# A four-layer mixture of experts on one core: the next layer's first weights scaled by ScalarE and split by VectorE one expert at a time, and the bias sums moved to another bank

## The reference, cut to what matters

```python
def _moe_layer(x, rw, rb, g, b, w1, b1, w2, b2):
    probs = softmax(einsum('bsh,he->bse', x, rw) + rb)
    vals, idx = top_k(probs, 2);  vals = vals / vals.sum(axis=-1, keepdims=True)
    xhat = normalized x (mean 0, variance 1 over h)
    xe = xhat[None] * g[:, None, None, :] + b[:, None, None, :]
    h = gelu(einsum('ebsh,ehf->ebsf', xe, w1) + b1[:, None, None, :])
    y = einsum('ebsf,efh->ebsh', h, w2) + b2[:, None, None, :]
    return sum over e of comb[e] * (x + y[e])     # comb: vals of the chosen two, else 0
for l in range(4): x = _moe_layer(x, rw[l], ..., b2[l])
```

## Time and profile before

| what | us |
|---|---|
| median of 3 runs (2304.45 to 2312.71) | 2306.93 |
| the profiled execution: its own time | 2305.76 |
| its span, first to last instruction | 2303.9 |
| TensorE busy in the span | 2152.2 (93%) |
| VectorE busy | 2023.0 (88%) |
| ScalarE busy | 1515.3 (66%) |
| GpSimd busy | 957.7 (42%) |
| expert stage, from TensorE's first product of it | some 916 |

### The profile page before, as it was taken

One profiled execution on the slowest core, in us unless ns is written; L12 is line 12 of the kernel. 1 busy time (PEld: TensorE's weight loads), 2 busy tenths in 40 slices (PEclk: granted clock), 3 DMA queues, 4 the chain that ended last, 5 costly groups with the idle time before them and its releaser, 6 DMA issues. The chain is left out here.

```text
span 2303.9 us, 49912 instructions
## 1 busy us (share of the span) xinstructions
PE 2152.2 (93%) x16960; PEld 1272.2 (55%) x16960; DVE 2023.0 (88%) x2878; ACT 1515.3 (66%) x1794; POOL 957.7 (42%) x464
## 2 busy tenths in 40 slices
PE   7887999999999999999999998998999999989987
PEld 3342333333333333333333347987899889989976
DVE  5768999999999999999999997777877877787776
ACT  4767888888888888888888873433344334434432
POOL 3224344443434444344434434444444544444442
PEclk9986999999999999999999999998999999999998
DMA  5886122212222221212222133000100010000000
GB/s 171 242 247 176 40 46 41 45 39 49 42 45 46 41 46 39 45 41 48 44 42 46 41 105 110 1 0 0 38 1 0 2 37 0 0 1 6 5 9 19
DMA packets 354955, 114.91 MB, mean 50 GB/s; under 512 B 283000, under 2 KB 345600, under 8 KB 354624
## 3 DMA queue, kind: packets, MB, share of 16 engines
q1 hardware_dynamic: 350416, 110.92, 19.6%
q10 hardware_dynamic: 4464, 3.02, 0.4%
HBM read 67.98 MB, written 45.88 MB: 49 GB/s over the span
## 5 line engine op out<-in xcount | busy, mean ns | idle before, releaser
L1492 DVE TENSOR_TENSOR_SCAN arena<-behind 128x1040 f32<-128x1040 f32 x512 | 1156.9, 2309 | 7.8 <-ACT behind L971 5.1
L1040 ACT ACTIVATE arena<-PS,arena 128x512 f32<-128x512 f32 x512 | 348.7, 688 | 545.6 <-PE PS L1272 544.7
L961 ACT ACTIVATE behind<-PS 128x1024 f32<-128x1024 f32 x512 | 526.7, 1029 | 133.8 <-DVE arena L1492 101.8
L1175 PE MATMUL PS<-arena 128*32 128x128 f32 x8192 | 566.2, 407 | 0.0
L971 ACT ACTIVATE behind<-PS 128x1024 f32<-128x1024 f32 x512 | 539.1, 1053 | 7.5 <-PE PS L1158 3.8
L1284 PEld LDWEIGHTS PS<-arena 128*128 128x128 f32 x4096 | 472.7, 192 | 8.1
L1284 PE MATMUL PS<-arena 128*128 128x128 f32 x4096 | 473.2, 275 | 0.0
L1272 PE MATMUL PS<-parts_xh,parts_w 128*128 128x512 f32 x1536 | 395.5, 411 | 46.1 <-DVE parts_xh L1654 20.2
L765 POOL COPY behind<-carry 128x64 f32<-128x64 f32 x128 | 209.1, 1633 | 517.1 <-DVE arena L1492 381.9
L1175 PEld LDWEIGHTS PS<-arena 128*32 128x32 f32 x8192 | 234.9, 119 | 287.5 <-issue 210.4
L1158 PE MATMUL PS<-arena 96*128 96x512 bf16 x1024 | 314.4, 389 | 53.5 <-ACT behind L971 39.4
(11 more groups left out here) (126 smaller groups left out, 1392.5 us busy)
## 6 DMA issues: line engine op xcount, KB each, us to landing
dl_d<-arena SPq DMA_DIRECT2D x48, 256.0 KB, 3.0
du_d<-arena SPq DMA_DIRECT2D x48, 256.0 KB, 3.3
arena<-dl_d SPq DMA_DIRECT2D x512, 24.0 KB
arena<-b_d SPq DMA_DIRECT2D x64, 192.0 KB
arena<-du_d SPq DMA_DIRECT2D x512, 24.0 KB
b_d<-arena SPq DMA_DIRECT2D x48, 128.0 KB, 2.8
u_d<-behind SPq DMA_DIRECT2D x8, 512.0 KB, 4.0
sz_d<-arena SPq DMA_DIRECT2D x8, 512.0 KB, 4.7
```

The costliest lines, as they stand in the source:

```text
L961: nc.scalar.activation(seg(dA[:, half])[:, :, 1:], PS[:, 0:2, :].rearrange("p j (i t) -> p (j i) t", t=TC), ACT.Exp).then_inc(exp_done, 1)
L1040: nc.scalar.activation(hT[:, e % 2, c], PS[:, HIDDEN[(GT * e + c) % 3], :], ACT.Gelu, bias=bias1[:, lp, e * GT + c:e * GT + c + 1]).then_i ...
L1175: last = nc.tensor.matmul(PS[32 * j:32 * j + 32, 4 + kk, 0:DB], cd[:, pair, j, 32 * i:32 * i + 32], seg(hb[kk])[:, :, 1 + 16 * j + i], sta ...
L1492: nc.vector.tensor_tensor_scan(hb[kk][:, q * QD * SEG:(q + 1) * QD * SEG], dA[:, q % 2], dB[:, G_, lo:lo + QD * SEG], 0.0, ALU.mult, ALU.a ...
```

## The change

ScalarE scales the next layer's w1, GpSimd does so no more. In the loop of a layer, turn g2 = 0, 1, 2, ScalarE scales expert g2 in the turn's first step (ahead of the gelus of expert 1), and VectorE splits it in the turn's second step, behind add_expert(2). Expert 3 is scaled and split in the last step, at the same places. The bias sums go to bank 7 (`Y_BANK[E - 1]`), which holds expert 3's result: `bias_of_offset` therefore waits for f_sum of all experts of the step before, and the wait for f_bias stands ahead of second(3). `add_bias` stands behind `stage_scores`. In a layer's first step TensorE waits for the first expert's split ahead of first(0) and for all four behind it.

```diff
         def run_layers(eng, begin, step):
             def layer(at_layer, following):
-                step(at_layer, 0, 0, None, True)
+                step(at_layer, 0, 0, None, True, None, None)
                 with eng.Fori(0, NG // 2 - 1) as g2:
                     for gp in range(2):
-                        step(at_layer, g2 * 2 + gp + 1, 1 - gp, None, True)
-                step(at_layer, NG - 1, 1, following, following is not None)
+                        make = (following, g2) if following else None
+                        step(at_layer, g2 * 2 + gp + 1, 1 - gp, None, True, make if gp == 0 else None,
+                             make if gp == 1 else None)
+                make = (following, E - 1) if following else None
+                step(at_layer, NG - 1, 1, following, following is not None, make, make)
...
-            def prepare(l, pair, lp):
...
-                for e in range(E):
-                    nc.gpsimd.tensor_tensor(w1g[:, e], w1_s[lp][:, e],
-                                            g_s[:, bass.ds(l * E + e, 1)].broadcast_to([P, F]), ALU.mult
-                                            ).then_inc(f_g, 1)
...
+            def scale_w1(at_layer, e):
+                l, pair, lp = at_layer
+                act.wait_ge(f_w[lp], F_LOADS * (pair + 1))
+                act.wait_ge(f_wp, E * l)
+                apart(act)
+                nc.scalar.activation(expert(w1g, e), expert(w1_s[lp], e), ACT.Identity,
+                                     scale=g_s[:, bass.ds(l * E + e, 1)]).then_inc(f_g, 1)
...
                 for e in range(E):
+                    if scale and e == 1:
+                        scale_w1(*scale)
...
-            def bias_of_offset(l, pair, lp):
+            def bias_of_offset(l, pair, lp, n):
 
                 pe.wait_ge(f_w[lp], F_LOADS * (pair + 1))
+                pe.wait_ge(f_sum, FS0 + E * n)
                 for ec in range(E * GT):
                     e, c = ec // GT, ec % GT
-                    last = nc.tensor.matmul(PS[:, 5, ec:ec + 1], w1_s[lp][:, e, c * P:(c + 1) * P],
+                    last = nc.tensor.matmul(PS[:, Y_BANK[E - 1], ec:ec + 1], w1_s[lp][:, e, c * P:(c + 1) * P],
                                             lb_s[:, bass.ds(l * E + e, 1)], start=True, stop=True)
                 last.then_inc(f_bp, 1)
-                pe.wait_ge(f_bias, l + 1)
...
-                if isinstance(g, int) and g == 0:
-
-                    pe.wait_ge(f_wp, l * E + E)
+                starts = isinstance(g, int) and g == 0
+                if starts:
+                    pe.wait_ge(f_wp, l * E + 1)
                 pe.wait_ge(f_xhTs, n + 1)
                 first(n, lp, gp, 0)
+                if starts:
+                    pe.wait_ge(f_wp, l * E + E)
...
+                if new:
+                    pe.wait_ge(f_bias, new[0] + 1)
                 second(n, lp, 3)
...
+            def split_w1(at_layer, e):
+
+                l, pair, lp = at_layer
+                dve.wait_ge(f_g, E * l + e + 1)
+                apart(dve)
+                nc.vector.tensor_copy(expert(w1p[:, lp, 0], e), expert(w1g, e)).then_inc(f_upper, 1)
+                dve.wait_ge(f_upper, E * l + e + 1)
+                apart(dve)
+                nc.vector.tensor_tensor(expert(w1p[:, lp, 1], e), expert(w1g, e),
+                                        expert(w1p[:, lp, 0], e).bitcast(fp32), ALU.subtract).then_inc(f_wp, 1)
...
-                if new:
-                    add_bias(next_l, next_lp)
                 if more:
                     stage_norm(n + 2, (g + 2) % NG, gp)
...
                     stage_scores(n + 1, next_l)
+                if new:
+                    add_bias(next_l, next_lp)
                 add_expert(n, g, gp, 1)
...
                 add_expert(n, g, gp, 2)
-                if new:
-                    split_w1(next_l, next_lp)
+                if split:
+                    split_w1(*split)
                 if more:
                     sum_bias(n + 1)
```

More of the change, by code:

```diff
@@ L807, in _ @@
             run_blocks(pool, emit)
-            def prepare(l, pair, lp):
-                pool.wait_ge(f_w[lp], F_LOADS * (pair + 1))
-                if not isinstance(l, int) or l > 0:
-                    pool.wait_ge(f_wp, E * l)
-                for e in range(E):
-                    nc.gpsimd.tensor_tensor(w1g[:, e], w1_s[lp][:, e],
-                                            g_s[:, bass.ds(l * E + e, 1)].broadcast_to([P, F]), ALU.mult
-                                            ).then_inc(f_g, 1)
             def stage_exp(n):
@@ L860, in begin, with step @@
                 pool.wait_ge(x_in, 16)
-            def step(layer, g, gp, new, more):
+            def step(layer, g, gp, new, more, scale, split):
                 n = layer[0] * NG + g
@@ L866, in step @@
                     stage_scores(n + 1, 0 if new else g + 1, new[0] if new else layer[0])
-                if new:
-                    prepare(*new)
                 if more:
@@ L1028, in _, with expert, step @@
             act.dma_start(b2_s, b2.rearrange("p (l e h) -> p l e h", l=NL, e=E)).then_inc(b2_in, 16)
-            def step(layer, g, gp, new, more):
+            def expert(v, e):
+                return v[:, bass.ds(e, 1)].rearrange("p a f -> p (a f)")
+            def scale_w1(at_layer, e):
[5 more added lines that the diff above has]
+                                     scale=g_s[:, bass.ds(l * E + e, 1)]).then_inc(f_g, 1)
+            def step(layer, g, gp, new, more, scale, split):
                 l, pair, lp = layer
@@ L1306, in step @@
                 if new:
-                    bias_of_offset(*new)
+                    bias_of_offset(*new, n)
                 first(n, lp, gp, 1)
@@ L1522, in lower_w1, with expert @@
                                             ).then_inc(f_wp, 1)
-            def split_w1(l, lp):
-                upper_w1(l, lp)
-                lower_w1(l, lp)
+            def expert(v, e):
+                return v[:, bass.ds(e, 1)].rearrange("p a f -> p (a f)")
+            def split_w1(at_layer, e):
[7 more added lines that the diff above has]
+                                        expert(w1p[:, lp, 0], e).bitcast(fp32), ALU.subtract).then_inc(f_wp, 1)
             dve.wait_ge(scan_done, NB * NQ)
@@ L1658, in add_bias @@
                 dve.wait_ge(f_bp, l + 1)
-                nc.vector.tensor_tensor(bias1[:, lp], PS[:, 3 if first else 5, 0:E * GT], b1_s[:, bass.ds(l * E * GT, E * GT)],
+                nc.vector.tensor_tensor(bias1[:, lp], PS[:, 3 if first else Y_BANK[E - 1], 0:E * GT], b1_s[:, bass.ds(l * E * GT, E * GT)],
                                         ALU.add).then_inc(f_bias, 1)
```

## The result

The changed kernel takes **2319.91 us** (median of 7 runs, 2317.66 to 2325.47), the kernel before 2306.93: ratio 1.0058, 95% interval 1.0043 to 1.0074. It is slower by 13.0 us; 10.5 were forecast. The profiled execution took 2317.66 us, its span is 2315.8 us against 2303.9: 11.9 us more.

A forecast was written before the change was run, and what follows sets the result against it. VectorE's chain with GpSimd, not TensorE, was taken to bound the kernel. 2305.76 us + 9.0 (loop copies) + 1.5 (last steps) = 2316.3, and the median 1.2 above the profiled execution gave 2317.4 us; range 2306 to 2322 (8 in 10).

The forecast's parts named there:

- The bound: Inside a layer, VectorE's chain with GpSimd sets the time: VectorE's step takes 26.62 us, TensorE's 25.70.
- D: Time mark from which a layer's last step is counted: the end of add_expert(3) of the step before.
- Rival D: TensorE sets the end, so its removed waits count: faster, -9.3 us in sum, 2297.6 us; chance 0.09.
- The copies in the loop: Nine VectorE copies ahead of sum_bias, held until GpSimd's L843 ends: +1.0 us each, +9.0 in all (8.1 to 11.3).
- Rival C: The loop's copies are not held, fit in the 2.31 us wait and cost nothing: 2308.4 us; chance 0.12.
- The last step: Three last steps: bias sums at half clock delay second(0) and take back VectorE's gain; +0.5 us each, +1.5 in all.
- Rival B: Clock comes back during the bias sums, first(1) at full clock: -2.8 us per last step, 2307.6 us; chance 0.14.
- The wait that took the stall's place: TensorE's wait ahead of the bias sums in the last step: 8.0 us in layers 1 and 2.
- ScalarE: Twelve scalings of 0.71 us ahead of expert 1's gelus, covered by TensorE's 0.9 us less work per step: cost zero.
- Rival E: ScalarE's scaling or longer register work is on the path: 9 x 0.7 us more, 2324 us; chance 0.05.

The follow-up runs named there:

- bank5_late: bank5 with TensorE waiting for f_bias only ahead of the transposes of the next x-hat, not ahead of first(1); 2297.53 us.
- bank5: The changed kernel with only its bias part undone: sums in bank 5 ahead of D, f_bias wait ahead of first(1), add_bias first in VectorE's last step; 2299.41 us.
- split_behind: The changed kernel with split_w1 behind sum_bias in place of ahead of it, in all 12 places; 2321.27 us.
- act_scale: The kernel before with only the scaling moved from GpSimd to ScalarE, all four experts in the last step; 2296.22 us.
- warm_fit: warm with the number of useless products fitted: 48 in layer 0, 32 in layers 1 and 2; 2310.50 us.
- pool_sub: bank5_late with ScalarE making the upper part too and GpSimd the subtraction, VectorE splitting nothing; 2285.68 us.
- warm: The changed kernel with 48 useless 128x512 products ahead of TensorE's wait for f_sum in each last step; 2312.67 us.
- warm_mixed: warm_fit with one useless 128x512 product behind each but the last of the 16 bias products; 2316.50 us.

## Why the prediction was right

**The bound.** VectorE's chain with GpSimd, not TensorE: right. The changed kernel took away TensorE's three waits for the split, 14.8 us, and became 13 us slower. bank5_late started first(1) 5.7 to 8.5 us earlier against D than bank5 and stood 10.9 us for the split again, and its last steps are the same to 0.02 us. Rival D falls.

**The copies in the loop.** Forecast 1.0 us each, 9.0 in all; measured 1.1 on average (the nine steps take 27.71 to 27.89 us, where 26.63 was usual), 10.1 in all, and the copy 2.64 us where I said about 2.6. Most of the missing 0.1 is the gap between copy and subtraction: 0.24 to 0.26 us in the loop, not 0.05. In the three last steps, where the awaited value is a constant and does not come from a register, the same gap is 0.14 to 0.15 us; that the register is the reason is likely but not shown. The mean of 1.1 lay within the bounds (0.9 to 1.25). Rival C falls: the nine copies took 2.63 to 2.65 us, each step became longer, and split_behind shows that it is GpSimd's product that holds them.

**The last step.** Forecast: sums 6.7 us at the low clock, second(0) at D + 15.6, last step 33.85. Measured: 6.96 us in all three; D + 16.3, 15.1 and 16.1; 34.60, 33.40 and 34.39. The forecast is 0.3 us below the mean, 0.8 in all. Most of it lies ahead of first(1), which starts at D + 6.97 in all three where I had 6.8; for first(1) and second(0) together I had 8.8, and 9.3, 8.1 and 9.1 are 8.8 on average. The spread of 1.2 us goes with the moment at which the clock comes back (12.7, 10.1 and 12.3 us behind the restart), and my bounds had covered it. That GpSimd's multiplies would give VectorE 3 us and TensorE take them back was right (act_scale, bank5). Rival B falls: in the changed kernel the clock did not come back during the sums, and warm_fit shows it even falling in them.

**The wait that took the stall's place.** Forecast 8 us in layers 1 and 2 and 12 in layer 0: 8.35, 8.26 and 13.02.

**ScalarE.** Forecast zero; in the trace of the changed kernel TensorE's first(0) and first(1) together took some 5.93 us in place of 5.71 in the steps with a scaling, under the cover of its lead. bank5's loop steps cost what the copies cost, 27.7 us, and nothing besides. Rival E falls.

The terms measured, 10.1 + 2.3 = 12.4, stand against 10.5 forecast, 11.9 between the spans and 13.0 between the medians. So both terms were somewhat too small, and the mechanism is the one that was forecast.

## What to carry to other kernels

The engine that waits longest at a boundary need not be the one to help: compare the length of the steps in the undisturbed middle of the loop, and follow the engine with the longer one. A wait of VectorE for a GpSimd instruction was no free slot for such a copy (2.31 us of waiting, and 1.1 us lost each time), since the copy was held until that instruction ended; in pool_sub the work went to other engines, at a time when VectorE reads PSUM or reduces, and cost nothing. And work that stands behind a wait of TensorE can run at the half clock that the wait leaves behind, as here behind each wait of 6.5 to 13 us, so small work belongs ahead of it.

## What the runs showed of the hardware that was not expected

TensorE's clock fell with thin products (128x1, fp32, 32 passes) although the engine was busy. The earlier trace rows had shown it once, ahead of the prediction. warm shows it with the engine busy on both sides: the granted clock went from 1.00 to 0.50 behind the sums with PE at 1.00 in every row. It fell in or right behind the sums in all six last steps of warm and warm_fit, and with a 128x512 product between each two thin ones it stayed at 1.00 in all three of warm_mixed. I had not expected that after 48 wide products directly ahead of the sums first(1) would still run at the low clock. The Trainium skill (TensorE: Matmul & The Clock Gate, "What's actually happening") has activity release the throttle; by these rows an engine that is busy throughout can lose its clock all the same.

The thin products also stood ahead of a later return of the clock. In bank5, where first(1) is the first work behind the wait, the clock was back 3.0, 3.9 and 5.0 us behind the restart in layers 0, 1 and 2; in the changed kernel, where the sums are first, it took 12.7, 10.1 and 12.3 us. Layer 1 of bank5, restart at 1817.95:

```profile
1821.00:1822.00 1.00, 1.00 (x4) 0.73 (x4) 1.00 (x1) 0.61 (x1) 1.00 (x1) 0.56 0.00 0
1822.00:1823.00 1.00, 1.00 (x8) 0.86 (x7) 1.00 (x1) 0.86 (x2) 1.00 (x1) 1.00 0.00 0
```

GpSimd's subtraction into the fp32r format took 1.27 us for 128x512.
